# A graph layer's stores of h and of the output, moved from SyncE's queue to ScalarE's

## The reference, cut to what matters

```python
h = jnp.maximum(_layernorm(x, axis=-1), 0.0)        # x: 8192 x 512, float32
mask = adj > 0                                      # adj: 8192 x 8192, float32, nearly all zeros
head = mask / jnp.maximum(jnp.sqrt(jnp.sum(mask * mask, axis=-1, keepdims=True)), EPS)
inc = adj + head
return x + (inc @ h) / jnp.sum(inc, axis=-1, keepdims=True)
```

## Time and profile before

| what | us |
|---|---|
| median of 3 runs | 1341.62 (1336.1 to 1348.91) |
| the profiled execution's own time | 1334.34 |
| its span, from first to last instruction | 1332.6 |
| busy in the span: DVE | 1168.8 |
| busy in the span: ACT | 978.6 |
| busy in the span: PE | 940.4 |
| moved by DMA | 469.14 MB, 352 GB/s on average |

### The profile page before, as it was taken

One profiled execution on the slowest core, in us unless ns is written; L12 is line 12 of the kernel. 1 busy time (PEld: TensorE's weight loads), 2 busy tenths in 40 slices (PEclk: granted clock), 3 DMA queues, 4 the chain that ended last, 5 costly groups with the idle time before them and its releaser, 6 DMA issues.

```text
span 1332.6 us, 14627 instructions
## 1 busy us (share of the span) xinstructions
PE 940.4 (71%) x2670; PEld 457.0 (34%) x2670; DVE 1168.8 (88%) x2845; ACT 978.6 (73%) x1905; POOL 777.0 (58%) x746
## 2 busy tenths in 40 slices
PE   0000887867887887787887888887788878788634
PEld 0000343333443443333443333443343433343312
DVE  5549999889989999898999899999799899898253
ACT  5447886878887887887888787778788788787321
POOL 1002567556676667576667675666666666677413
PEclk9999999899998999998899988989999989999677
DMA  8999999999999999999999999999999999996321
GB/s 346 336 353 406 396 375 376 340 377 356 380 390 345 377 393 388 377 388 373 385 392 389 372 391 375 390 377 376 383 397 391 388 388 388 383 382 227 108 84 42
DMA packets 147390, 469.14 MB, mean 352 GB/s; under 512 B 24752, under 2 KB 24752, under 8 KB 143149
## 3 DMA queue, kind: packets, MB, share of 16 engines
q1 hardware_dynamic: 89792, 330.33, 64.5%
q0 software_dynamic: 57504, 137.85, 28.7%
HBM read 488.64 MB, written 33.82 MB: 392 GB/s over the span
## 4 chain that ended last, share of the span: by engine, by line
DVE 63%; issue 18%; DMA 6%; another core or an unknown queue 5%; ACT 5%; POOL 1%; PE 1%; DVEq 0%; SPq 0%; ACTq 0%; POOLq 0%
DVE cand_word L742 21%; DVE folded L720 21%; DVE cand_index L746 8%; DMA h_scratch<-gathered_rows 5%; ACT gathered_rows L520 2%; ACT junk L533 1%; DVE diagonal_alone L727 1%; DVE entry L878 1%; DVE folded L736 1%; DVE weights_and_payload L841 1%; DMA adj_tile<-in_adj_dram,bad_row_number 1%; DVE entry_sign L784 1%; DVE inc L829 1%; ACT diag L592 1%
## 5 line engine op out<-in xcount | busy, mean ns | idle before, releaser
L454 POOL DMA_INDIRECT gathered_rows<-h_scratch,slot_column x520 | 559.6, 1076 | 310.9 <-issue 159.0
L1157 PE MATMUL acc<-gathered_rows,diag 128*128 128x512 f32 x1040 | 494.6, 620 | 90.3 <-DMA gathered_rows<-h_scratch,slot_column 74.7
L533 ACT ACTIVATE junk<-adj_tile,zero_unit 128x2048 bf16<-128x2048 f32 x256 | 509.9, 2000 | 4.9 <-DMA adj_tile<-in_adj_dram 4.9
L454 POOL DMA_INDIRECT gathered_rows<-h_scratch,spill_column x195 | 208.5, 1069 | 227.3 <-ACT spill_column L575 163.5
L1157 PEld LDWEIGHTS acc<-gathered_rows,diag 128*128 128x128 f32 x1040 | 197.3, 197 | 339.0 <-issue 338.8
L742 DVE MAX8 cand_word<-folded 128x8 f32<-128x1024 f32 x256 | 312.8, 1222 | 0.5 <-issue 0.3
L746 DVE FIND_INDEX8 cand_index<-cand_word,folded 128x8 uint32<-128x1024 f32 x256 | 312.2, 1219 | 0.0
L720 DVE SCALAR_TENSOR_TENSOR folded<-adj_tile 128x1024 f32<-128x1024 f32 x256 | 310.9, 1215 | 0.0
L1165 PE MATMUL acc<-gathered_rows,spill_matrix 128*128 128x512 f32 x390 | 220.6, 711 | 90.8 <-DMA gathered_rows<-h_scratch,spill_column 74.1
L592 ACT ACTIVATE diag<-ident,weights_and_payload 128x128 f32<-128x128 f32 x584 | 177.3, 387 | 32.7 <-issue 17.6
L1165 PEld LDWEIGHTS acc<-gathered_rows,spill_matrix 128*128 128x128 f32 x390 | 81.7, 223 | 181.2 <-issue 181.2
(11 more groups left out here) (152 smaller groups left out, 860.2 us busy)
## 6 DMA issues: line engine op xcount, KB each, us to landing
adj_tile<-in_adj_dram SPq DMA_DIRECT2D x256, 1024.0 KB
h_scratch<-gathered_rows SPq DMA_DIRECT2D x16, 1024.0 KB, 8.9
out_dram<-out_tile SPq DMA_DIRECT2D x64, 256.0 KB
gathered_rows<-in_x_dram SPq DMA_DIRECT2D x11, 1024.0 KB, 7.3
x_residual<-in_x_dram SPq DMA_DIRECT2D x44, 256.0 KB
gathered_rows<-h_scratch,slot_column POOLq DMA_INDIRECT x520
x_held<-in_x_dram SPq DMA_DIRECT2D x5, 1024.0 KB, 8.1
gathered_rows<-h_scratch,spill_column POOLq DMA_INDIRECT x195
```

Source lines behind the costliest of these rows:

```text
L454: nc.gpsimd.indirect_dma_start(out=into, out_offset=None, in_=h[:, :], in_offset=bass.IndirectOffsetOnAxis(ap=column, axis=0), bounds_chec ...
L533: nc.scalar.activation(junk[:, n % 2].rearrange("p (j c) -> p j c", j=2), both[:, :, half], ACT.Relu, bias=zero_unit[:], scale=-UP, accum_ ...
L1157: last = nc.tensor.matmul(acc[t % 3][:], diag[:, t % 2, 1 + s], slot(t % 2, s), start=False, stop=False)
```

## The change

`ln_store` and `store_tile` leave SP's program and enter ACT's. ACT issues the store of chunk c right behind `ln_apply(c)`, after a wait on its own completion count `ln_done`, and the store of a finished tile behind `finish_tile` and `roots`, after a wait on `out_ready`. At the end each of the last three stores stands right behind its `finish_tile`. SP issues loads alone: 16 loads of x, then all chunks of `adj` with the residual rows between. Sizes, buffers and the bytes moved are the same.

```diff
             for c in range(4):
                 ln_load(c)
             for c in range(4, LN):
-                ln_store(c - 4)
                 ln_load(c)
-            load_chunk(0, 0)
-            for c in range(LN - 4, LN):
-                ln_store(c)
-                if c < LN - 1:
-                    load_chunk(0, c - (LN - 4) + 1)
+            for j in range(CHUNKS):
+                load_chunk(0, j)
...
-                if t >= 4:
-                    store_tile(t - 4)
                 if t >= HELD:
                     load_x(t)
...
-            for t in range(TILES - 4, TILES):
-                store_tile(t)
...
+            def ln_store(c):
+                act.wait_ge(ln_done, c + 1)
+                act.dma_start(h_ln[c], hst(c % 2)).then_inc(h_stored[c % 2], 16)
+
+            def store_tile(t):
+                act.wait_ge(out_ready, t + 1)
+                act.dma_start(out_t[t // ROWS, t % ROWS], osb[:, t % 2]).then_inc(out_stored[t % 2], 16)
...
                 if p >= 0:
                     roots(p)
+                if f >= 0:
+                    store_tile(f)
                 if q >= 0:
                     copy_owner(q)
...
                 ln_apply(c)
+                ln_store(c)
...
             finish_tile(TILES - 3)
+            store_tile(TILES - 3)
             spill_matrix(TILES - 1)
             finish_tile(TILES - 2)
+            store_tile(TILES - 2)
             for k in range(4):
                 check_batch(k)
             finish_tile(TILES - 1)
+            store_tile(TILES - 1)
```

More of the change, by code:

```diff
@@ L340, in ln_load @@
                 sp.dma_start(xin(c), x_ln[c]).then_inc(ln_loaded[c % 8], 16)
-            def ln_store(c):
-                sp.wait_ge(ln_done, c + 1)
-                sp.dma_start(h_ln[c], hst(c % 2)).then_inc(h_stored[c % 2], 16)
             def load_chunk(t, j):
@@ L357, in load_x @@
                 sp.dma_start(xres[:, t % 2], x_t[t // ROWS, t % ROWS]).then_inc(x_loaded[t % 2], 16)
-            def store_tile(t):
-                sp.wait_ge(out_ready, t + 1)
-                sp.dma_start(out_t[t // ROWS, t % ROWS], osb[:, t % 2]).then_inc(out_stored[t % 2], 16)
             for c in range(4):
```

## The result

The changed kernel takes 1356.2 us (median of 4 runs, 1346.8 to 1360.7), the kernel before 1338.9 us beside it: the ratio is 1.0115, with a 95% interval from 1.0067 to 1.0163. The forecast was 1341.6 and no change; the time lies inside the range of 1324 to 1360, but the change is a loss, and a sure one. The profiled execution took 1346.8 us with a span of 1345.0, 12.4 us more than the span before, and was the fastest of the four, so its rows show somewhat less than the whole loss.

What follows compares the result with a forecast made beforehand. Bound: stage one waits for transfers; stage two is a nearly full DVE beside a ring of `finish_tile`, `spill_columns`, gather, product. 1334.3 - 10 + 10 + 0 = 1334.3, plus 7.3 to the runs' median: 1341.6 us, range 1324 to 1360.

Steps and rivals of the forecast that it cites:

- The ring's case: Rival, stage two: each period longer by ACT's whole store issue, PE meeting every gather waiting; 1360.1 us, chance 0.14.
- The signs named for stage two: Gap `finish_tile` to `spill_columns` 1.14 to 1.6 us; POOL's waits up to 20 us more, `find_entry`'s about 10 more.
- The step that failed: Stage two: of 19.8 us of later gathers only half costs, since PE waited for spill gathers 33 times in some 64.
- the bounds 0 and 28.5: Stage two's cost in us: 0 if all is covered, 28.5 if 62 periods each pay 0.46.
- The whole term: Stage two: tile stores issued on ACT delay `spill_columns` and the gathers behind it, +10 us.
- Stage one: Start of the kernel: h stores in a queue apart from the loads shorten the staging buffers' turns, -10 us.
- the landing: Stage one: h store's time from issue to landing, median 8.9 us, expected to fall to about 7; bounds 4.8 and 8.9.
- The tail: End of the kernel: three stores on ACT, 1.4 us of issue, counted as 0, at most 1.4 us.
- The bytes beside the gathers: Stage two: a tile store's 256 KB shares the engines with spill gathers, 0.65 us, put inside the upper bound.
- ScalarE hiding its issues: Rival: stage one gains its 10 us, stage two loses nothing; 1331.6 us, chance 0.25.
- Nothing gained in stage one: Rival: loads and stores share the DMA engines, landing stays at 8.9 us, ACT pays as forecast; 1351.6 us, chance 0.10.
- Fewer stalls: Rival, stage two: residual rows and `adj` land earlier, some 20 us of DVE's stalls go; 1321.6 us, chance 0.07.

Runs made afterwards that it cites:

- e9: Kernel before, plus a wait for `out_ready` and one unused ACT copy ahead of `copy_owner`, no store moved: 1.0121 of the kernel before, slow chip.
- e13: Changed kernel with `spill_columns` ahead of `finish_tile` and each tile's store behind `spill_matrix`: 0.9831 of the kernel before, slow chip.
- e14: e11 plus a wait for `out_ready` and one unused ACT copy ahead of `copy_owner`: 0.9752 of the kernel before, slow chip.
- e10: Changed kernel with `spill_columns` moved ahead of `finish_tile`, all stores still on ACT: 0.9866 of the kernel before, slow chip.
- e11: e10 with the finished tiles' stores back on SP, h stores on ACT: 0.9779 of the kernel before, slow chip.
- e4: Changed kernel with each tile's store issued one period later, directly ahead of the next `finish_tile`: 0.9996 of the kernel before, fast chip.
- e1: Changed kernel with the finished tiles' stores back on SP, only h stores on ACT: 0.997 of the kernel before, fast chip.
- e3: Kernel before, plus a wait for `out_ready` and one unused ACT copy ahead of `copy_owner`, no store moved: 0.9989 of the kernel before, fast chip.
- e15: Same kernel as e1, run again on a slow chip: 0.9956 of the kernel before.

## Why the prediction was wrong

**The bound** was read rightly: a ring of `finish_tile`, `spill_columns`, gather and product beside a DVE that is nearly full, and ACT's idle time ahead of `finish_tile` as no cover for what comes behind it. The ring's case was written down as a rival with a chance of 0.14. Two rows of that reading were short: the waits of `find_entry` are 65.2 us in 18, with the rows for `pbrought` and "issue", and ACT's for the product 106.0 us with the row for PE. The signs named for stage two came as forecast, the gap at 1.55, POOL's waits 7.4 us longer and those of `find_entry` 10.0 us longer; it was their price that was wrong.

**The step that failed** is the one that halves the cost: "A later gather costs only where PE then waits for it: PE waited for spill gathers 33 times in some 64, about half." It takes the waits of the old trace as fixed while the delay is put in. The cleanest measure is e9, which has the delay and no moved store: that rule gives 9 us for 0.42 us (half of 43 times it), and 16 came through. The likely reason is that a period in which PE doesn't wait, or in which DVE releases `spill_columns`, has a little slack, and the same delay, added every period, uses that up: the 13 releases by DVE became 5, POOL's 43 waits 52. How much of it is this and how much the clock of the product was not separated. The whole term was +10 and measured 20.2 in the profile, the stores' own cost included. The delay itself was sized well, 0.46 forecast and 0.41 measured, and of the bounds 0 and 28.5 the upper one was the nearer. Adding 0.41 times 62 periods, 25 us, whole would have been 5 off instead of 10.

**Stage one** was right in kind, wrong in size: -10 forecast, -3.9 at the first mark of this profile and 5.4 by the averages of all profiles. The mis-sized piece is the landing. It fell from 8.9 to 8.4 us, near the upper bound and not the lower, and with it the pace of 5.4 us a chunk, taken from bytes at 406 GB/s, was out of reach: two chunks are a landing of 8.4, four operations of 2.93 and some 0.3, 11.6 us, and between 46.99 and 87.53 us seven chunks took 5.8 us each. The rate from 20 to 80 us, forecast near 390 GB/s, is 346, no more than before. Then DVE, which was ready 6.1 us earlier, lost 2.2 of it again waiting for the first chunks of `adj`.

**The tail** was counted at 0 and is 3.9 us shorter in the profile. No experiment was made on that, and it need not be the change's doing: in e9, whose end is that of the kernel before, it is 130.4 us, as short as here (129.8 against 133.7).

**The bytes beside the gathers** were put "inside the upper bound". e13 against e14 gives them, or whatever else goes with ACT's queue, 0.8%, e10 against e11 0.9%, and e4 against e1 0.26% on the fast chip. This was a second term, and it was missing from the sum.

**The rivals.** ScalarE hiding its issues is out, on the slow chips; on the fast one the delay is hidden (e3 shows no change), though the tile stores still cost 0.48% there. Nothing gained in stage one is out: e1 and e15 gain 0.3 and 0.4%. Fewer stalls is out: 75 us of waits in `find_entry` where there were 65. The ring, at 1360.1, is 4 us above the time measured, which is partly luck: it had 6 us too much gain in stage one and 8 too much loss in stage two.

**The rules of the Trainium skill.** That issuing from several engines saves only the sequencer's time ("DMA: Bandwidth & Descriptors", "Issuing engines are not separate DMA queues") would have given 0 in stage one, and the h stores gain 0.3 to 0.4%. That doesn't refute it, since the change did more than use a second issuer: SP's loads no longer stand behind its waits for `ln_done`, and no run tells this from the separate queue. What the rule leaves out is the other side: on an engine with work in order behind it, that time is paid there, 0.34 us of issue and 0.07 of wait in each period here.

**A better version** than both came of it: `spill_columns` ahead of `finish_tile`, h stores on ACT, tile stores on SP (e11), 0.9779 of the kernel before on a slow chip. On the fast chip it wasn't run.

## What to carry to other kernels

A DMA issued by a compute engine costs its issue time where it stands in that engine's order, and is free only if nobody waits for what stands behind it: look at the release, not at the engine's busy share. A small delay repeated in every turn of a loop with several near-equal bounds shouldn't be scaled by how often the old trace shows a wait; more came through here than that share, 16 us of 26 where it said 9. A product that stands behind a long wait can also run at half the clock (5.46 us instead of 2.81 here), so in such a loop count the matmuls' time after the wait as well as the wait. When such a loop shows up, look for an operation that stands in it only by program order; taking that out was worth more here than all that the change moved.

## What the runs showed that I had not expected

The same kernel before takes 1287.6 us on one chip and 1335 to 1339 on others, 3.6% apart, and the effect of one and the same edit, e3 and e9, goes from none (0.9989) to 1.0121 between them. The cause is open; the transfers' own time differs by about 1%, and the spill matmuls at the lower clock are 18 to 39 there and 77 to 120 on the others. A result about slack holds for the chip on which it was measured.

GpSimd's own busy time rose from 777.0 to 799.2 us with the same 715 gathers, and fell to 747.3 in e10: the time that a gather's issue takes isn't fixed. The stores' queue isn't what sets it: e9, with all stores on SP, has 798.9, and the four kernels with `spill_columns` ahead have 747 to 752 wherever the stores are. An issue of 1.86 us stands in the period shown above, where most take 1.00. What does set it was not tried.
